# Pitch of the phase rows in SBUF: 528 elements in place of 514

## The reference

```python
x = x + L0(x)   # grouped conv1d, 4 groups, 9 taps, pad 4, + context + bias
x = x + L1(x)   # per-sample 128x128 matrix: softmax mix of 8 matrices, + bias
x = x + L2(x)   # the same with other weights
x = x + L3(x)   # grouped conv1d as L0, with other weights
```

## Time and profile before

| | |
|---|---|
| median of 3 runs | 661.62 us (661.17 to 661.68) |
| span of the profiled execution | 658.9 us |
| TensorE (PE) busy | 648.5 us, 98% |
| PE weight loads, beside the matmuls | 591.5 us, 90% |
| VectorE (DVE) busy | 476.4 us, 72% |
| ScalarE (ACT) busy | 263.7 us, 40% |
| GpSimd (POOL) busy | 242.3 us, 37% |
| DMA, queue of SyncE | 54.2% of 16 engines' span |

### The profile page before, as it was taken

One profiled execution on the slowest core, in us unless ns is written; L12 is line 12 of the kernel. 1 busy time (PEld: TensorE's weight loads), 2 busy tenths in 40 slices (PEclk: granted clock), 3 DMA queues, 4 the chain that ended last, 5 costly groups with the idle time before them and its releaser, 6 DMA issues.

```text
span 658.9 us, 24674 instructions
## 1 busy us (share of the span) xinstructions
PE 648.5 (98%) x11218; PEld 591.5 (90%) x11218; DVE 476.4 (72%) x948; ACT 263.7 (40%) x332; POOL 242.3 (37%) x87
## 2 busy tenths in 40 slices
PE   8999999999999999999999999999999999999995
PEld 6889999999999999999999999999999999999995
DVE  7997877677677677677677677677677677677635
ACT  5743423433423433423433423433423433423424
POOL 4024433442433442433442433442433442433220
PEclk9999999999999999999999999999999999999999
DMA  7355676545466545466545466545566545554425
GB/s 236 98 166 180 201 226 225 165 155 203 149 223 223 164 155 202 148 223 223 163 156 200 150 223 223 164 155 199 151 223 223 161 158 199 153 163 161 144 83 193
DMA packets 50325, 118.77 MB, mean 180 GB/s; under 512 B 5557, under 2 KB 26090, under 8 KB 42474
## 3 DMA queue, kind: packets, MB, share of 16 engines
q1 hardware_dynamic: 49026, 116.56, 54.2%
q10 hardware_dynamic: 1064, 1.61, 0.8%
q0 software_dynamic: 192, 0.02, 0.0%
HBM read 35.33 MB, written 33.55 MB: 105 GB/s over the span
## 4 chain that ended last, share of the span: by engine, by line
PE 95%; DVE 2%; DMA 1%; ACT 1%; issue 0%; DVEq 0%
PE ps L894 79%; PE ps L964 14%; PE ps L951 1%; DMA out_sb<-in_L_cond_weight 1%; PE ps L932 1%; DVE x_in L777 1%; DVE x_planes L780 0%; DVE x_hi L820 0%; DVE acc L718 0%; DVE mat L718 0%; ACT L616 0%; PE ps L1002 0%; ACT x_planes L566 0%; PE ps L944 0%; DVE taps_raw L738 0%
## 5 line engine op out<-in xcount | busy, mean ns | idle before, releaser
L417 POOL COPY out_sb<-out_planes 128x2048 f32<-128x2048 f32 x30 | 118.6, 3954 | 220.4 <-DVE mat2T L718 208.4
L408 POOL COPY x_planes<-x_in 128x2048 f32<-128x2048 f32 x29 | 112.8, 3889 | 137.4 <-DVE x_lo L665 137.4
L485 ACT ACTIVATE y_hi<-ps,bias_tab 128x512 fp32r<-128x512 f32 x128 | 77.5, 689 | 188.4 <-PE ps L894 188.4
L689 DVE SCALAR_TENSOR_TENSOR z_lo<-ps,bias_tab,z_hi 128x1024 fp32r<-128x1024 f32 x62 | 76.8, 1280 | 68.7 <-ACT z_hi L495 68.6
L679 DVE SCALAR_TENSOR_TENSOR y_lo<-ps,bias_tab,y_hi 128x512 fp32r<-128x512 f32 x128 | 87.2, 744 | 38.4 <-ACT y_hi L485 38.4
L894 PE MATMUL ps<-z_hi,taps_lo 32*128 32x512 f32 x1488 | 99.3, 397 | 0.0
L894 PE MATMUL ps<-x_lo,taps_hi 32*128 32x512 f32 x1536 | 96.6, 391 | 0.0
L894 PE MATMUL ps<-x_hi,taps_hi 32*128 32x512 f32 x1536 | 96.0, 390 | 0.1
L894 PE MATMUL ps<-x_hi,taps_lo 32*128 32x512 f32 x1536 | 96.1, 389 | 0.0
L503 ACT ACTIVATE out_taps<-ps,bias_tab 128x512 f32<-128x512 f32 x62 | 39.3, 684 | 133.9 <-PE ps L894 133.9
L894 PE MATMUL ps<-z_hi,taps_hi 32*128 32x512 f32 x1488 | 92.8, 391 | 0.0
(11 more groups left out here) (124 smaller groups left out, 553.1 us busy)
## 6 DMA issues: line engine op xcount, KB each, us to landing
x_in<-in_x SPq DMA_DIRECT2D x31, 1024.0 KB, 5.1
out_planes<-out_taps SPq DMA_DIRECT2D x122, 256.0 KB, 2.5
out<-out_sb SPq DMA_DIRECT2D x30, 1024.0 KB, 4.5
mix_w<-prod SPq DMA_DIRECT2D x126, 128.0 KB, 3.6
x_in<-in_x SPq DMA_DIRECT2D x2, 512.0 KB, 5.0
out<-x_planes SPq DMA_DIRECT2D x7, 128.0 KB, 2.7
out_taps<-in_L_cond_weight SPq DMA_DIRECT2D x1, 512.0 KB, 5.3
mix_w<-in_L_cond_weight SPq DMA_DIRECT2D x1, 512.0 KB, 6.5
```

The costliest lines, as they stand in the source:

```text
L408: pool.tensor_copy(x_planes[:, :, :], planes(x_in[t.par(d)], slice(0, S))).then_inc(x_planed, 1)
L417: pool.tensor_copy(out_sb[t.par(d)][:, :].rearrange("c (s p) -> c p s", p=PH), out_planes[:, :, :])\
L485: act.activation(y_hi[:, g, :], ps[:, bank(t, 0) + g, :], ACT.Identity, bias=bias_tab[:, b, g:g + 1]).then_inc(y_hi_done, 1)
L689: dve.scalar_tensor_tensor(out=z_home(t, 0)[1][:, 2 * h:2 * h + 2, 1:S + 1], in0=ps[:, k:k + 2, :], scalar=bias_tab[:, b, 2 * G:BIAS], in1 ...
```

## The change

The phase rows of `x_hi`, `x_lo`, `z_hi` and `z_lo` get a pitch of 528 elements (2112 bytes, 33 times 64) in place of 514 (2056 bytes, 32 times 64 and 8 more). All instructions, their shapes and their order are the same; the columns 514 to 527 are never touched. Each buffer grows from 8224 to 8448 bytes for each partition, and everything that is allocated after the first one moves.

```diff
+ROW = 528
-        x_hi = [sb(f"x_hi{i}", [C, PH, S + 2], F32R) for i in range(2)]
-        x_lo = [sb(f"x_lo{i}", [C, PH, S + 2], F32R) for i in range(2)]
+        x_hi = [sb(f"x_hi{i}", [C, PH, ROW], F32R) for i in range(2)]
+        x_lo = [sb(f"x_lo{i}", [C, PH, ROW], F32R) for i in range(2)]
         y_hi = sb("y_hi", [C, G, S], F32R)
         y_lo = sb("y_lo", [C, G, S], F32R)
-        z_hi = sb("z_hi", [C, PH, S + 2], F32R)
-        z_lo = sb("z_lo", [C, PH, S + 2], F32R)
+        z_hi = sb("z_hi", [C, PH, ROW], F32R)
+        z_lo = sb("z_lo", [C, PH, ROW], F32R)
```

## The result

The changed kernel takes 663.58 us (median of 7 runs, 663.32 to 663.72); the kernel before, beside it, 661.61 us (7 runs, 661.17 to 662.0). The ratio is 1.0027, with a 95% interval of 1.0018 to 1.0037. It is slower by 2.0 us, a little more than the 1.3 us that the prediction gave as the measurement's limit. No change was forecast. The 663.58 us lie inside the range of the prediction (659.3 to 664.4), near its slow end.

The account below looks back on a forecast made before the run. TensorE's slots were taken to bound the kernel; reads, writes and moves each added 0 to the 658.9 us span, which stands 2.7 us below the median, so the forecast was 661.6 us, range 659.3 to 664.4.

Parts of the forecast that it names:

- What bounds the kernel: TensorE sets the time by its slots; one nanosecond per convolution slot, 2304 in all, is 2.3 us.
- my signs for the chain: TensorE's steady stretch if the forecast is right: 216 matmuls in 12.5 to 12.6 us, 48 of `mix` in 2.80.
- Writes, start, end: ScalarE and VectorE writes and the start-up casts cost nothing; start at most 0.24 us either side; the end scales.
- the reads: TensorE's reads of value rows: 576 of 2304 slots go from crossing to aligned, costed at 0 ns.
- the moves: Buffers behind the enlarged ones shift by 896 or 1344 bytes; costed at 0.
- I take the nearest row, mix, and cost the alignment at nothing: TensorE reads: aligned `mix` slots take 233.3 ns, mostly unaligned convolution slots 232.9, so alignment was costed at nothing.
- both bounds of the sum: Limits for the convolution reads: gain 4.8 us if all match the quickest pass, loss 0.9 us if all match `mix`.
- Everything behind the buffers ... keeps its place in a 64-byte line. Cost: nothing: `y`, `out_taps` and weights move by 14 or 21 times 64 bytes, keeping their place in a line; cost nothing.
- The 64-byte lines: Rival: TensorE reads pay for each 64-byte line, so 576 aligned slots gain 4.2 us; 657.4 us, chance 0.07.
- Equal places take the quick slots away: Rival: equal starts hold slots at 389 ns; signs no spread, medians 389+, 12.66 us or more; 665.3 us, chance 0.12.
- The pattern is dealt anew: Rival: single convolution slots get a new pattern, 1 ns either side; 659.3 us (0.09) or 663.9 us (0.08).
- The rule of the Trainium skill: SBUF reads pay per 16-byte line crossed; 4 of 12 taps begin on one before and after, so 0 us.

Follow-up runs that it names:

- all_64: The kernel before with 64 unused bytes ahead of its first buffer, so every buffer moves together; 661.44 us, ratio 0.9995.
- pad_only: The kernel before, pitch kept at 514, with only the six value buffers enlarged to their size with 528; 655.42 us, ratio 0.991.
- row_576: The changed kernel with a pitch of 576 elements in place of 528; 659.82 us, ratio 0.9971 to the kernel before.
- pad_taps_64: pad_only with 64 unused bytes ahead of the tap weights, so all weights move against the values; 663.95 us, ratio 1.0037 to the kernel before.
- row_544: The changed kernel with a pitch of 544 elements in place of 528; 660.27 us, ratio 0.9982 to the kernel before.

## Why the prediction was wrong

**What bounds the kernel** held. TensorE's slots set the time; 1 ns per convolution slot is 2.3 us. The measured +1.4 ns makes the +3.2 us of the convolutions. But both of my signs for the chain failed: 12.66 us and not 12.5 to 12.6, and 2.76 us for `mix` and not 2.80.

**Writes, start, end** held. ScalarE and VectorE rows moved by less than 1%, and no new wait appeared in the steady stretch. The new wait of 0.8 us in the start-up is more than my 0.24, but all_64 has it without the pitch, so it isn't a price of the change.

**Two terms of the sum failed**, both put at nothing: the reads and the moves. At equal places the pitch cost +8.2 us (the change against pad_only), and the moves were worth -6.1 us (pad_only against the kernel before). They nearly cancel, and only by that luck did the time stay within 2.0 us of the forecast and inside the range.

**"I take the nearest row, mix, and cost the alignment at nothing"** is the step that had the reads wrong. `mix` was taken for a sample of aligned reads in general. It was a sample of distance 192, the worst of the four at a pitch of 514: at distance 0 it takes 227.5 (pad_only) to 230.8 ns (row_576). In pad_only, where both groups have distance 0, its slots are 3.5 ns shorter than those of the convolutions (227.5 and 231.0); before, its worse distance hid that. Whether the 3.5 ns are the price of unaligned reads or of rows that step from tap to tap, no run shows. But aligned reads of stepping rows did not come out quicker: 528 has more of them than 514 and is slower at equal places. The +8.2 us are outside both bounds of the sum (-4.8 to +0.9), and so are the +2.0 of both terms together. The upper bound was also read too low, from one sample: over 24 samples the `z_hi` pass with high weights takes 234.0 ns a slot in the kernel before, which would have made it 1.1 x 2304 = 2.5 us.

**"Everything behind the buffers ... keeps its place in a 64-byte line. Cost: nothing"** is the step that had the moves wrong. I costed a move of 896 and 1344 bytes by the one unit of the diff. Nothing in the rows said that 64 bytes is the unit that TensorE sees. The moves, those of the value buffers among them, are worth -6.1 us, and it is a move against the weights that counts (pad_taps_64, all_64), not one in itself.

**The rivals.** The 64-byte lines fall: taps 0 to 3 aren't all near 383 ns, and row_544 with the same places in a line is 3.3 us quicker than 528. The three thirds of the `z_lo` pass in the changed kernel (the last two with one tap of the neighbour):

```profile
L895 PE MATMUL ps<-z_lo,taps_hi x16: 386/388/392, 223.2 to 223.9; 32*128 32x512 f32 x16
L895 PE MATMUL ps<-z_lo,taps_hi x20: 387/392/399, 223.9 to 224.9; 32*128 32x512 f32 x20
L895 PE MATMUL ps<-z_lo,taps_hi x20: 388/396/398, 224.9 to 225.8; 32*128 32x512 f32 x20
```

Reads that begin on the boundary are the quickest third here, but they aren't at 383, and the loss is in the other two. "Equal places take the quick slots away" came near in size for the convolutions (1.6 ns forecast, 1.4 measured) and two of its three signs showed: 12.66 us for 216 matmuls, and medians of 392 and 394 ns, above 389. The third did not: no slot is held at 389, the spread is as wide as before. Its cause is wrong as well: row_544 has the same places in a line, and its convolutions are quicker (12.60 us for 216 matmuls). "The pattern is dealt anew" is what happened: both `x_hi` buffers have one pattern now, as that rival said, and 663.6 us lies 0.3 us from its slow side (663.9). That nearness is luck: I gave that side 8 in 100 and took 1 ns for its width, from passes at six distances that average out. With one distance for all buffers, they don't: pad_only and pad_taps_64 are 3 ns apart.

**The rule of the Trainium skill**, 16-byte lines ("SBUF — State Buffer", "Door 1: The DMA port swizzle"), counts as many aligned taps before as after and gave 0 us; the pitch of 516 costs 4.9 us over 514 at equal places, where 4 of 12 taps begin on a 16-byte line with either pitch and its count gives no loss. In pad_taps_64 no read changes its place in such a line, and 8.5 us were lost. The measurement decides: lines of 16 bytes don't order these times.

**What stays open.** That value rows and weights meet in SBUF is my reading of the distance; no run shows the meeting itself. Nor do I know why 528 is slower than 514 at distances 0 and 128, which is the very loss of this change, or how the history of the slots enters. pad_only is the best version found: 655.42 us, 0.9% under the kernel before and 1.2% under the change, for 1344 bytes of unused SBUF for each partition.

## What to carry to other kernels

When TensorE sets the time, the SBUF addresses of values and weights are a parameter that can be tried: gaps of 64, 128 and 192 bytes between them, one run each, before changing a layout. Here they were worth up to 8.5 us of 655. A change of a buffer's size moves all that is behind it, so time the padding alone beside the change that needs it. And a group that serves as a reference for a cost must be like the changed one in everything else that its rows vary with; if single instructions repeat to the nanosecond and yet differ from each other, the cause can be looked for by moving one thing at a time, as here, though part of it stayed open.

## What the runs showed of the hardware

- A slot of four matmuls of 32 rows by 512 columns took between 227.5 ns (`mix` in pad_only, 2.73/12) and 234.3 ns (convolutions of the change) at a clock of 0.997 and more, for the same instructions, by addresses alone.
- At a pitch of 514, with one distance for all value buffers, the time depended on the distance between value buffers and weights modulo 256 bytes: 655.4, 658.3, 658.3 and 664.0 us for 0, 64, 128 and 192 (and 655.8 us with the weights 256 bytes further). Moving all buffers together by 64 bytes changed nothing (ratio 0.9995).
- The durations of tap 0 were the same in the kernel before and in all_64, which has equal distances (383 and 389 ns for the two `x_hi` buffers); all slots of the passes in the table above agree to 1 ns between two kernels of one distance and pitch.
- The busy time of the weight loads beside the matmuls ran from 557.5 (all_64) to 640.0 us (row_576) and didn't go with the time (661.4 and 659.8 us).
- The pitch of the rows that they write cost ScalarE and VectorE nothing that shows: 1112 and 1115 ns, 1280 and 1281 ns. Their writes begin at element 1 with either pitch, so this says nothing of an odd place.
